# First attention of a four-layer kernel: value bias folded into the output bias, weights rounded on GpSimd, sixteen unread products between the halves of the norm

## The chip, the cores and the metric

The kernel runs on one core of a Trainium2 chip. The metric is the device time of one execution in microseconds. The kernel is timed in runs of its own, and one more execution is recorded by the profiler; times inside the kernel are counted from the start of the span of that execution.

## The reference

Four layers run one after the other, each with a layer norm before it and a residual sum behind it. Only the first matters here:

```python
x = x + attn0(layernorm(x), Wqkv, bqkv, Wo, bo)      # x: 1024 x 512
x = x + ffn0(layernorm(x), w1, m1, w2, m2, w3, m3)   # base + mean(|w - base|) * sign(w - base)
x = x + attn1(...)                                    # 32 heads, index scores, top 128
x = x + ffn1(...)                                     # LoRA

def attn0(x, Wqkv, bqkv, Wo, bo):                     # one head of 128
    q, k, v = split(x @ Wqkv + bqkv)
    p = softmax(q @ k.T / sqrt(128))
    return (p @ v) @ Wo + bo
```

Since the rows of the softmax sum to one, the value bias adds `bv @ Wo` to every row of the result.

## The kernel before, in words

All matrix products are made to float32 accuracy by splitting each operand into a rounded part and a rest (`hi`, `lo`), and adding three products (`mm3`: L345, L346, L347 in order of issue). One operand pair costs two operations: the rounding (ScalarE, or a CAST on VectorE) and a subtraction (VectorE, L1086 in `split`, or GpSimd).

Five engine programs run side by side, each in its own written order, and meet through semaphores.

- SyncE loads x (8 tiles of 128 rows), the attention's weights and biases, and then 44 chunks of feed-forward weights, two loads to a chunk. The chunks go through a ring of four slots: a slot is loaded again when ScalarE is done with the chunk in it.
- GpSimd subtracts the base from each chunk (L582). It does nothing else up to the second layer.
- ScalarE takes the sign (L771) and the sum of absolute values (L773) of each chunk in `weight_chunk`. Between these it rounds the transposed tiles of the norm (L761), adds the query and key biases (L790), rounds the values (L818), takes the exponentials of the scores (L809) and rounds their transposes (L823).
- VectorE does the norm in two halves of four tiles (`first_norm`: statistics, a square root on ScalarE at L779, then L1071 to L1079, then one scaling a tile at L1103), splits the projection weights tile by tile between these, takes the row maxima of the scores, and the rests of all operands. It also splits the output weights (`W0`) and adds the output bias to x (`B0`, `B4`).
- TensorE transposes the normed tiles (L1522), makes the query and key projections (4 groups of 12 products of 512 columns), then goes through `ATT_PE`: `S` a tile of scores, `V` a value tile (two bias products at L1539, then 12 of 128 columns), `T` the eight transposes of a tile of probabilities (L1584), `O` probabilities times values, `Y` the output projection. Before `T7` it waits until ScalarE has done 28 chunks (L1568), since the sum over these scales the first feed-forward weights.

The three lists `ATT_PE`, `ATT_ACT` and `ATT_DVE` are written by hand; in `ATT_ACT`, `Cn` stands for n weight chunks.

## Time and profile before

| | |
|---|---|
| three timed runs, median | 1443.37 us (1441.29 to 1444.63) |
| profiled execution | 1442.61 us |
| its span | 1440.8 us |
| TensorE busy | 1329.5 us (92%) |
| VectorE busy | 1107.4 us (77%) |
| ScalarE busy | 832.9 us (58%) |
| GpSimd busy | 641.7 us (45%) |

PE is TensorE's matmul stream, PEld its weight loads, DVE VectorE, ACT ScalarE, POOL GpSimd, SPq the queue that issues transfers. A row of the timeline has the start, the duration, engine, line, operation, what is written and read, and the count; in brackets stands the idle time before it and what ended it. [...] Busy time of pipelined matmuls overlaps, so the distance from one start to the next is the better measure of pace.

### The profile page before, as it was taken

To read this page: it belongs to the slowest core of one execution; us is meant where nothing else is said; L and a number is where in the kernel's file an instruction comes from. 1 tells how busy PE (TensorE), PEld (TensorE's weight loads), DVE (VectorE), ACT (ScalarE), POOL (GpSimd) and SP (SyncE) were. 2 spreads that over 40 slices of the span, in tenths; PEclk is the share of its full clock that TensorE was granted. 3 is DMA by queue.
4 is the path that set the end of the run, shared out by engine and by line. 5 is a ranking of instruction groups with operands and counts; after the bars stand their busy time and mean duration, and the time that the engine had idled before them with its cause. 6 is when DMAs were issued, how large, how long until landed. Compare 5 with 4: busy or idle time off the path is not lost.

```text
span 1440.8 us, 21299 instructions
## 1 busy us (share of the span) xinstructions
PE 1329.5 (92%) x7160; PEld 1107.8 (77%) x7160; DVE 1107.4 (77%) x2247; ACT 832.9 (58%) x1819; POOL 641.7 (45%) x630
## 2 busy tenths in 40 slices
PE   3988999999899689998769999999999999999998
PEld 2776888888789677776448888888888888888886
DVE  6567334443648499999979988988899889898976
ACT  4663542233246557774567667666776766677661
POOL 3520210010037445654665555556655655566534
PEclk9887999999999899998669999999999999999999
DMA  6630310000122334754830000000000000000021
GB/s 225 207 99 27 102 52 1 0 20 0 39 65 69 97 73 129 233 168 137 276 119 14 1 28 29 28 29 28 1 28 29 28 28 28 28 16 14 15 81 59
DMA packets 83722, 95.59 MB, mean 66 GB/s; under 512 B 11680, under 2 KB 59296, under 8 KB 83104
## 3 DMA queue, kind: packets, MB, share of 16 engines
q1 hardware_dynamic: 83616, 94.24, 20.9%
q8 instruction: 59, 0.97, 0.3%
q14 instruction: 47, 0.39, 0.1%
HBM read 75.34 MB, written 18.87 MB: 65 GB/s over the span
## 4 chain that ended last, share of the span: by engine, by line
PE 71%; DVE 16%; ACT 4%; issue 3%; DMA 2%; POOL 1%; SPq 1%; DVEq 0%; ACTq 0%
PE ps L345 17%; PE ps L347 16%; PE ps L346 16%; PE ps L1851 9%; PE ps L1871 3%; PE ps L1870 3%; DVE acc L1376 3%; DVE top L1387 2%; DVE xn_l L1449 1%; DVE rop L1399 1%; DVE acc L1390 1%; DVE rop L1397 1%; DVE pm L1429 1%; DVE rop L1398 1%; PE ps L1551 1%
## 5 line engine op out<-in xcount | busy, mean ns | idle before, releaser
L717 POOL TENSOR_SCALAR pm<-pm,smx 128x128 f32<-128x128 f32 (+1 forms) x255 | 188.8, 749 | 208.5 <-DVE smx L1436 208.5
L1024 ACT ACTIVATE pm<-pm,smx 128x128 f32<-128x128 f32 (+7 forms) x256 | 197.4, 773 | 35.5 <-DVE smx L1429 34.6
L1429 DVE CUSTOM_DVE_ANT_0 pm<-ps,mbias 128x128 f32<-128x128 f32 (+7 forms) x256 | 191.5, 752 | 29.0 <-PE ps L1851 13.4
L1851 PE MATMUL ps<-ident,pm 128*128 128x128 f32 x1152 | 174.8, 277 | 7.1 <-DVE pTa_l L1449 2.0
L1030 ACT ACTIVATE xn_h<-ps 128x512 fp32r<-128x512 f32 (+3 forms) x256 | 128.4, 512 | 84.5 <-PE ps L1851 81.5
L1449 DVE TENSOR_TENSOR xn_l<-ps,xn_h 128x512 fp32r<-128x512 f32 (+3 forms) x256 | 144.4, 587 | 24.2 <-ACT xn_h L1030 23.2
L345 PE MATMUL ps<-latT_l,qc_h 128*128 128x512 f32 (+3 forms) x384 | 143.1, 373 | 17.0 <-DVE smx L1429 8.9
L1851 PEld LDWEIGHTS ps<-ident,pm 128*128 128x128 f32 x1152 | 132.8, 141 | 32.9 <-issue 11.4
L347 PE MATMUL ps<-latT_h,qc_h 128*128 128x512 f32 (+3 forms) x384 | 134.0, 349 | 0.0
L346 PE MATMUL ps<-latT_h,qc_l 128*128 128x512 f32 (+3 forms) x384 | 133.6, 348 | 0.0
L1376 DVE SCALAR_TENSOR_TENSOR acc<-ps,iw,acc 128x768 f32<-128x768 f32 (+4 forms) x105 | 87.1, 875 | 25.3 <-ACT ps L910 25.1
L345 PEld LDWEIGHTS ps<-latT_l,qc_h 128*128 128x128 f32 x384 | 73.2, 191 | 34.0 <-issue 13.0
L678 POOL TENSOR_TENSOR rop<-rop 128x512 f32<-128x512 f32 x60 | 77.3, 1288 | 36.6 <-DVE rop L1399 36.6
L345 PE MATMUL ps<-xn_l,wc 128*128 128x512 f32 x224 | 91.9, 410 | 0.0
L582 POOL TENSOR_TENSOR wring<-wring,base 128x512 f32<-128x512 f32 (+1 forms) x33 | 43.1, 1309 | 108.4 <-DMA wring<-in_L_ffn_w 108.1
L1870 PE MATMUL ps<-xn_l,v 128*128 128x512 f32 (+3 forms) x256 | 91.3, 362 | 0.0
L1390 DVE MATCH_REPLACE8 acc<-top,acc 128x640 f32<-128x640 f32 (+4 forms) x112 | 89.7, 809 | 0.0
L346 PE MATMUL ps<-xn_h,wc 128*128 128x512 f32 x224 | 89.3, 399 | 0.0
L347 PE MATMUL ps<-xn_h,wc 128*128 128x512 f32 x224 | 89.2, 398 | 0.0
L910 ACT ACTIVATE ps<-ps 128x640 f32<-128x640 f32 (+4 forms) x112 | 73.9, 690 | 26.2 <-PE ps L347 26.0
L345 PE MATMUL ps<-ikT_l,iqT_h 128*128 128x512 f32 (+3 forms) x176 | 66.1, 376 | 23.3 <-DVE acc L1376 22.1
L1871 PE MATMUL ps<-xn_h,v 128*128 128x512 f32 (+3 forms) x256 | 87.0, 358 | 0.0
(287 smaller groups left out, 3742.6 us busy)
## 6 DMA issues: line engine op xcount, KB each, us to landing
iwq_raw<-in_L_attn_idx_wq_w SPq DMA_DIRECT2D x48, 256.0 KB, 3.3
base<-in_L_ffn_mean_w SPq DMA_DIRECT2D x28, 256.0 KB, 3.2
wring<-in_L_ffn_w SPq DMA_DIRECT2D x21, 256.0 KB, 3.6
ow_raw<-in_L_attn_o_w SPq DMA_DIRECT2D x8, 512.0 KB, 4.0
xn_t<-in_L_attn_o_w SPq DMA_DIRECT2D x8, 512.0 KB, 4.1
wuvo<-pr_even SPq DMA_DIRECT2D x8, 512.0 KB, 5.2
wuvo<-pr_hl SPq DMA_DIRECT2D x8, 512.0 KB, 4.8
wuvo_h<-wuvo SPq DMA_DIRECT2D x16, 256.0 KB, 2.7
```

The costliest lines, as they stand in the source:

```text
L345: pe.matmul(dst, lh, rl, start=start, stop=False)
L346: pe.matmul(dst, ll, rh, start=False, stop=False)
L347: return pe.matmul(dst, lh, rh, start=False, stop=stop)
L717: pool.tensor_scalar(pm[:, i % 4, 0:w], pm[:, i % 4, 0:w], smx[:, 32 + i:33 + i], 0.0, ALU.mult, ALU.add).then_inc(hd_p, 1)
L1024: act.activation(pm[:, i % 4, 0:w], pm[:, i % 4, 0:w], ACT.Exp, bias=smx[:, i:i + 1], scale=-1.0, accum_out=smx[:, 16 + i:17 + i]).then_in ...
L1030: act.activation(dst[:, 4 * c:4 * c + nk, tile(tq % 4)], ps[:, t_bank(p, i), 0:nk * P].rearrange("p (k s) -> p k s", k=nk), COPY).then_inc ...
L1376: dve.scalar_tensor_tensor(acc_of(t), score(n, t), w, acc_of(t), ALU.mult, ALU.add)\
L1429: dve.tensor_tensor_reduce(out=pm[:, i % 4, 0:w], in0=two_banks(2 * (i % 2), w), in1=mbias[:, TRI[t]:TRI[t + 1]], scale=1.0, scalar=3.0 * BIG,
L1449: dve.tensor_tensor(dl[at], ps[:, t_bank(p, i), 0:nk * P].rearrange("p (k s) -> p k s", k=nk), f(dh[at]), ALU.subtract).then_inc(hd_lo, 1)
L1851: done = pe.transpose(ps[:, t_bank(p, i), tile(k)], pm[:, tq % 4, tile(4 * c + k)], ident[:])
L1870: pe.matmul(ps[:, 6, q], v, pl[:, k, q], start=k == 0, stop=False)
L1871: done = pe.matmul(ps[:, 6, q], v, ph[:, k, q], start=False, stop=k == nk - 1)
```

## The change

- The value bias is no longer put into the value tiles. GpSimd spreads it over 128 columns and splits it; TensorE multiplies it with the output weights (`Z0`, three products into bank 5), and VectorE adds the result to `bo_bc` (`B0`). The rows of x get that sum from GpSimd, in two runs of four additions before chunks 16 and 20.
- The projection weights and output weights are split on GpSimd, before chunks 4 and 7.
- The query and key projections are rounded by ScalarE from PSUM straight into `qkT_h`, and VectorE takes the rest with one operation from PSUM.
- Between tiles 3 and 4 of the norm, TensorE makes sixteen products of 512 columns into bank 7 that nothing reads.
- ScalarE does four chunks behind tile 3 and two behind tile 7 (before: one behind each of tiles 3 to 7), three instead of nine before the scores, and 19 instead of 14 in `ATT_ACT`.

```diff
@@ -78,10 +78,12 @@
     return [(step[0], int(step[1:])) for step in order.split()]
 
 
-ATT_PE = items("S0 S1 V0 V1 V2 V3 S2 V4 V5 V6 V7 T0 S3 T1 S4 T2 S5 T3 S6 O0 T4 S7 Y0 Y1 T5 Y2 T6 Y3 T7 O1 "
+ATT_PE = items("S0 S1 V0 V1 V2 V3 Z0 S2 V4 V5 V6 V7 T0 S3 T1 S4 T2 S5 T3 S6 O0 T4 S7 Y0 Y1 T5 Y2 T6 Y3 T7 O1 "
                "Y4 Y5 Y6 Y7")
-ATT_ACT = items("S0 S1 C2 V0 C2 S2 C1 V1 T0 C1 T1 S3 T2 S4 C1 T3 S5 C1 S6 C3 O0 T4 C1 S7 T5 C1 T6 C1 T7 O1")
-ATT_DVE = items("S0 S1 W0 V0 S2 B0 V1 T0 S3 T1 S4 T2 S5 T3 S6 B4 O0 T4 S7 Y0 Y1 T5 Y2 T6 Y3 T7 O1 Y4 Y5 Y6 Y7")
+ATT_ACT = items("C1 S0 S1 C2 V0 C1 S2 C2 V1 T0 C1 T1 S3 C1 T2 S4 C1 T3 S5 C2 S6 C2 O0 T4 C1 S7 C1 T5 C2 T6 C2 T7 O1")
+ATT_DVE = items("S0 S1 V0 B0 S2 V1 T0 S3 T1 S4 T2 S5 T3 S6 O0 T4 S7 Y0 Y1 T5 Y2 T6 Y3 T7 O1 Y4 Y5 Y6 Y7")
+FIRST_CHUNKS = {3: 4, 7: 2}
+ADD_AT = {16: 0, 20: 4}
 
 
 
@@ -418,8 +425,7 @@
             sp.dma_start(attn_raw[:, 0:NK * 3 * D0].rearrange("p (k n) -> p k n", k=NK),
                          wqkv.rearrange("(k p) n -> p k n", p=P)).then_inc(ld_a, 16)
             with nc.allow_non_contiguous_dma(reason="a small bias column"):
-                sp.dma_start(bq_col[:], bqkv[0:2 * D0].rearrange("(a p) -> p a", p=P)).then_inc(ld_a, 16)
-            sp.dma_start(bv_bc[:], row(bqkv[2 * D0:3 * D0], D0)).then_inc(ld_a, 16)
+                sp.dma_start(bq_col[:], bqkv.rearrange("(a p) -> p a", p=P)).then_inc(ld_a, 16)
             sp.dma_start(attn_raw[:, NK * 3 * D0:], wo).then_inc(ld_a, 16)
             sp.dma_start(bo_bc[:], row(bo, HID)).then_inc(ld_a, 16)
 
@@ -435,7 +441,7 @@
                     c = slice((s % 4) * 448, (s % 4) * 448 + 448)
                     ws, ms = rows[:, s // 4, c], mrows[:, s // 4, c]
                 if chunk == 2 * NI:
-                    sp.wait_ge(at_w, 2)
+                    sp.wait_ge(at_wo, 1)
                     sp.wait_ge(at_proj, 6)
                     sp.wait_ge(at_b, 2)
                 number, last, _ = RING[chunk]
@@ -575,9 +581,39 @@
                                pattern=[[-1, P]], channel_multiplier=1)
             pool.drain().then_inc(consts, 1)
 
+            def first_weights():
+                pool.wait_ge(ld_a, 64)
+                for k in range(NK):
+                    pool.tensor_copy(wqkv_h[:, k, :], raw[:, k, :])
+                pool.drain()
+                for k in range(NK):
+                    pool.tensor_tensor(wqkv_l[:, k, :], raw[:, k, :], f(wqkv_h[:, k, :]), ALU.subtract)
+                pool.drain().then_inc(at_w, 1)
+
+            def output_weights():
+                pool.tensor_copy(wo_h[:], attn_raw[:, NK * 3 * D0:])
+                pool.tensor_scalar(bv_f[:], ones[:], bq_col[:, 2:3], 0.0, ALU.mult, ALU.add)
+                pool.drain()
+                pool.tensor_tensor(wo_l[:], attn_raw[:, NK * 3 * D0:], f(wo_h[:]), ALU.subtract).then_inc(at_wo, 1)
+                pool.tensor_copy(bv_h[:], bv_f[:])
+                pool.drain()
+                pool.tensor_tensor(bv_l[:], bv_f[:], f(bv_h[:]), ALU.subtract).then_inc(at_bv, 1)
+
+            def bias_rows(first):
+                pool.wait_ge(at_zb, 1)
+                for t in range(first, first + 4):
+                    pool.tensor_tensor(xt(t), xt(t), bo_bc[:], ALU.add)
+                pool.drain().then_inc(at_b, 1)
+
             for chunk in range(WCHUNKS):
                 m, s, width = wt_chunk(chunk)
                 slot = ring(chunk)
+                if chunk == 4:
+                    first_weights()
+                elif chunk == 7:
+                    output_weights()
+                if chunk in ADD_AT:
+                    bias_rows(ADD_AT[chunk])
                 pool.wait_ge(ld_w[RING[chunk][0]], 32 * (RING[chunk][2] + 1))
                 pool.tensor_tensor(slot, slot, base[m][:, s * width:(s + 1) * width], ALU.subtract).then_inc(wt_d, 1)
 
@@ -779,20 +815,15 @@
                 act.activation(rs_sqrt[:, c], rs_var[:, c], ACT.Sqrt).then_inc(at_rs, 1)
                 for t in range(4 * half, 4 * half + 4):
                     norm_hi(0, t)
-                    if t >= 3:
+                    for _ in range(FIRST_CHUNKS.get(t, 0)):
                         weight_chunk()
-            for _ in range(4):
-                weight_chunk()
             for u in range(4):
+                m, n = divmod(u, 2)
                 act.wait_ge(at_proj, u + 1)
-                if u >= 2:
-                    act.wait_ge(at_qkv, u - 1)
-                act.activation(xn_t[:, u % 2, :], ps[:, u, :], ACT.Identity,
-                               bias=bq_col[:, u // 2:u // 2 + 1]).then_inc(at_q, 1)
-                if u < 2:
+                act.activation(qkT_h[:, m, 512 * n:512 * n + 512], ps[:, u, :], ACT.Identity,
+                               bias=bq_col[:, m:m + 1]).then_inc(at_q, 1)
+                if u < 3:
                     weight_chunk()
-            for _ in range(3):
-                weight_chunk()
 
             def weight_hi(g, k):
                 act.wait_ge(ff_tr, 2 * g + k + 1)
@@ -1111,8 +1142,6 @@
                 dve.tensor_scalar(rs_var[:, first:first + n], mv[:, first:first + n, 1], EPS, None, ALU.add)
                 rsqrt(k, n, first)
 
-            raw = attn_raw[:, 0:NK * 3 * D0].rearrange("p (k n) -> p k n", k=NK)
-
             def first_norm(half):
                 c = slice(4 * half, 4 * half + 4)
                 dve.wait_ge(ld_x[half], 64)
@@ -1136,17 +1165,14 @@
             for t in range(4, NT):
                 norm_scale(0, t)
                 norm_lo(0, t - 1)
-                if t == 4:
-                    dve.wait_ge(ld_a, 80)
-                split(wqkv_h[:, t - 4, :], wqkv_l[:, t - 4, :], raw[:, t - 4, :])
             norm_lo(0, NT - 1)
-            dve.drain().then_inc(at_w, 1)
             for u in range(4):
                 m, n = divmod(u, 2)
                 c = slice(512 * n, 512 * n + 512)
                 dve.wait_ge(at_q, u + 1)
-                split(qkT_h[:, m, c], qkT_l[:, m, c], xn_t[:, u % 2, :])
-                dve.drain().then_inc(at_qkv, 1)
+                dve.scalar_tensor_tensor(qkT_l[:, m, c], ps[:, u, :], bq_col[:, m:m + 1], f(qkT_h[:, m, c]),
+                                         ALU.add, ALU.subtract).then_inc(at_qkv, 1)
+
             def values(b):
                 dve.wait_ge(at_vhi, b + 1)
                 dve.tensor_tensor(v_l[:, 4 * b:4 * b + 4, :], ps[:, 6 + b, :].rearrange("p (k s) -> p k s", k=4),
@@ -1181,14 +1207,9 @@
                 if kind == "V":
                     values(i)
                     continue
-                if kind == "W":
-                    split(wo_h[:], wo_l[:], attn_raw[:, NK * 3 * D0:])
-                    dve.drain().then_inc(at_w, 1)
-                    continue
                 if kind == "B":
-                    for t in range(i, i + 4):
-                        dve.tensor_tensor(xt(t), xt(t), bo_bc[:], ALU.add)
-                    dve.drain().then_inc(at_b, 1)
+                    dve.wait_ge(at_z, 1)
+                    dve.tensor_tensor(bo_bc[:], bo_bc[:], ps[:, 5, :], ALU.add).then_inc(at_zb, 1)
                     continue
                 if kind == "O" and i == 1:
                     dve.wait_ge(wt_tot, 1)
@@ -1222,6 +1243,7 @@
                         for t in range(4):
                             norm_lo(1, t)
                 else:
+                    dve.wait_ge(at_b, i // 4 + 1)
                     dve.wait_ge(at_y, i + 1)
                     dve.scalar_tensor_tensor(xt(i), ps[:, 7 - i % 2, :], sm0[:, 3 * NT + i:3 * NT + i + 1], xt(i),
                                              ALU.mult, ALU.add).then_inc(at_x, 1)
@@ -1524,6 +1546,10 @@
 
             for t in range(NT):
                 norm_tile(0, t)
+                if t == 3:
+                    pe.wait_ge(ln_hi, 4)
+                    for _ in range(16):
+                        pe.matmul(ps[:, 7, :], xn_h[:, 0, 0:P], xn_h[:, 0, 0:512], start=True, stop=True)
             pe.wait_ge(ln_lo, NT)
             pe.wait_ge(at_w, 1)
             for u in range(4):
@@ -1536,10 +1562,9 @@
 
             def value_tile(t):
                 dst = ps[:, 6 + t // 4, tile(t % 4)]
-                pe.matmul(dst, ones[0:1, :], bv_bc[0:1, :], start=True, stop=False)
                 for k in range(NK):
                     last = mm3(pe, dst, xn_h[:, k, tile(t)], xn_l[:, k, tile(t)],
-                               wqkv_h[:, k, tile(2)], wqkv_l[:, k, tile(2)], False, k == NK - 1)
+                               wqkv_h[:, k, tile(2)], wqkv_l[:, k, tile(2)], k == 0, k == NK - 1)
                 if t % 4 == 3:
                     last.then_inc(at_proj, 1)
 
@@ -1561,6 +1586,11 @@
             for kind, i in ATT_PE:
                 if kind == "V":
                     value_tile(i)
+                    continue
+                if kind == "Z":
+                    pe.wait_ge(at_wo, 1)
+                    pe.wait_ge(at_bv, 1)
+                    mm3(pe, ps[:, 5, :], bv_h[:], bv_l[:], wo_h[:], wo_l[:], True, True).then_inc(at_z, 1)
                     continue
                 if kind == "T" and i == 7:
                     pe.wait_ge(wt_abs, 2 * NI)
@@ -1580,6 +1610,8 @@
                     pe.wait_ge(at_exp, i + 1)
                     for c in range(2):
                         reach(pe, at_lo, 2 * i + c - 1 if i else 0)
+                        if i == 0 and c == 1:
+                            pe.wait_ge(at_zb, 1)
                         for k in range(4):
                             last = pe.transpose(ps[:, 4 + c, tile(k)], p0[:, i % 3, tile(4 * c + k)], ident[:])
                         last.then_inc(at_tr, 1)
@@ -1601,8 +1633,6 @@
                             norm_tile(1, t)
                 else:
                     pe.wait_ge(at_ot, i // 4 + 1)
-                    if i == 0:
-                        pe.wait_ge(at_w, 2)
                     if i >= 2:
                         pe.wait_ge(at_x, i - 1)
                     mm3(pe, ps[:, 7 - i % 2, :], oT[:, 0, tile(i % 4)], oT[:, 1, tile(i % 4)], wo_h[:], wo_l[:],
```

## Rows read from the trace of the kernel before

**Rows 1.** Stretches of the span by stage: engines' busy time, clock, transfers.

```profile
49.68:78.00 28.32, 28.32 (x131) 24.57 (x132) 11.13 (x13) 14.28 (x29) 11.84 (x9) 0.66 0.49 149
78.00:109.63 31.63, 25.88 (x124) 19.99 (x122) 24.16 (x37) 26.28 (x53) 9.04 (x7) 0.88 0.41 126
...
128.00:380.00 252.00, 247.99 (x1152) 202.53 (x1151) 102.33 (x162) 85.55 (x167) 19.45 (x14) 0.99 0.09 25
```

**Rows 2.** Timeline from 17 to 34 us, all engines.

```profile
17.65 0.62 ACT L771 ACTIVATE sgn<-wring 128x512 int8<-128x512 f32 x1
...
19.60 1.26 POOL L582 TENSOR_TENSOR row_bc<-row_bc,base 128x512 f32<-128x512 f32 x1
...
20.33 0.56 DVE L1125 TENSOR_SCALAR rs_var<-mv 128x4 f32<-128x4 f32 x1
20.95 0.21 ACT L779 ACTIVATE rs_sqrt<-rs_var 128x4 f32<-128x4 f32 x1 [1.89 <-DVEq L1126]
...
30.69 1.27 POOL L582 TENSOR_TENSOR wring<-wring,base 128x512 f32<-128x512 f32 x1 [7.04 <-DMA wring<-in_L_ffn_w]
30.81 1.56 DVE L1086 TENSOR_TENSOR wqkv_l<-attn_raw,wqkv_h 128x384 fp32r<-128x384 f32 x1
...
31.65 0.62 ACT L771 ACTIVATE sgn<-wring 128x512 int8<-128x512 f32 x1
...
33.16 0.63 ACT L771 ACTIVATE sgn<-wring 128x512 int8<-128x512 f32 x1
33.17 0.77 PE L345 MATMUL ps<-xn_l,wqkv_h 128*128 128x512 f32 x1 [2.17 <-DVEq L1143]
```

**Rows 3.** Timeline of TensorE in the value tiles, at either clock.

```profile
52.62 0.48 PE L1539 MATMUL ps<-bv_bc,ones 1*128 1x128 f32 x2
...
53.03 0.33 PE L345 MATMUL ps<-wqkv_l,xn_h 128*128 128x128 f32 x1
...
54.31 0.27 PE L347 MATMUL ps<-wqkv_h,xn_h 128*128 128x128 f32 x1
...
71.00 0.79 PE L1539 MATMUL ps<-bv_bc,ones 1*128 1x128 f32 x2
...
74.47 0.79 PE L1539 MATMUL ps<-bv_bc,ones 1*128 1x128 f32 x2
```

**Rows 4.** Short stretches around changes of TensorE's pace and clock.

```profile
34.97:38.38 3.41, 3.41 (x9) 2.65 (x8) 0.00 (x0) 2.41 (x6) 2.27 (x2) 1.00 0.92 308
38.40:41.80 3.40, 3.40 (x16) 2.74 (x15) 1.00 (x2) 2.98 (x6) 2.33 (x3) 1.00 0.84 303
45.22:48.63 3.41, 1.75 (x8) 1.08 (x6) 3.10 (x4) 1.55 (x3) 1.49 (x2) 1.00 0.69 199
...
55.47:58.86 3.39, 3.39 (x27) 3.01 (x26) 1.64 (x2) 3.04 (x8) 2.62 (x2) 1.00 0.25 66
58.90:62.27 3.37, 3.37 (x15) 3.18 (x16) 0.15 (x1) 0.87 (x3) 1.28 (x1) 0.50 0.85 285
```

**Rows 5.** Timeline of TensorE where it waits for the chunks.

```profile
109.63 0.63 PE L1568 MATMUL ps<-absum,ones 128*128 128x28 f32 x2 [1.13 <-ACTq L774]
```

**Rows 6.** VectorE's groups by form, 22 to 50 us: busy us, mean ns, idle before.

```profile
L1086 DVE TENSOR_TENSOR wqkv_l<-attn_raw,wqkv_h 128x384 fp32r<-128x384 f32 x4 | 3.2, 808 | 0.3
...
L1084 DVE CAST wqkv_h<-attn_raw 128x384 fp32r<-128x384 f32 x4 | 1.4, 348 | 0.0
```

**Rows 7.** GpSimd's groups by form: busy us, mean ns, idle before.

```profile
L629 POOL CAST v<-latn 128x512 fp32r<-128x512 f32 x1 | 0.6, 613 | 0.0
```

**Rows 8.** ScalarE's groups by form, 78 to 109.63 us.

```profile
L823 ACT ACTIVATE xn_h<-ps 128x512 fp32r<-128x512 f32 x14 | 7.7, 596 | 2.3 <-PE ps L1584 1.9
L809 ACT ACTIVATE p<-ps,sm 128x1024 f32<-128x1024 f32 x5 | 5.6, 1116 | 1.4 <-DVE sm L1208 1.3
...
L809 ACT ACTIVATION_READ_ACCUMULATOR p<-ps,sm 128x1 f32 x5 | 1.0, 200 | 0.0
```

**Rows 9.** Timeline of TensorE in front of the first scores.

```profile
49.68 0.50 PE L345 MATMUL ps<-qkT_l,qkT_h 128*128 128x512 f32 x1 [2.71 <-DVEq L1149]
```

More of the change, by code:

```diff
@@ L184, in build @@
         wqkv_l = sbin(q_scope, "wqkv_l", [P, NK, 3 * D0], F32R)
+        bv_f = sbin(q_scope, "bv_f", [P, D0])
+        bv_h = sbin(q_scope, "bv_h", [P, D0], F32R)
+        bv_l = sbin(q_scope, "bv_l", [P, D0], F32R)
         q_scope.close()
@@ L194, in build @@
         v_l = sbin(a_scope, "v_l", [P, NT, D0], F32R)
-        bq_col = sbin(a_scope, "bq_col", [P, 2])
-        bv_bc = sbin(a_scope, "bv_bc", [P, D0])
+        bq_col = sbin(a_scope, "bq_col", [P, 3])
         wo_h = sbin(a_scope, "wo_h", [P, HID], F32R)
@@ L304, in build @@
         at_rv, at_rs, at_w, at_proj, at_q, at_qkv, at_vhi, at_v, at_b = sems("at_", "rv rs w proj q qkv vhi v b")
+        at_wo, at_bv, at_z, at_zb = sems("at_", "wo bv z zb")
         at_s, at_max, at_exp, at_tr, at_hi, at_lo = sems("at_", "s max exp tr hi lo")
@@ L353, in xt @@
             return x[:, t * HID:(t + 1) * HID]
+        raw = attn_raw[:, 0:NK * 3 * D0].rearrange("p (k n) -> p k n", k=NK)
         def two_banks(b, w=1024):
```

## The prediction

> **What bounds the kernel now.** I read the stages first [rows 1]: is TensorE full, and at which clock? From 128 to 380 us it is busy 247.99 of 252.00 us: behind the first attention it has no slack, so whatever the attention gives or takes by 128 us moves the end one for one. The change lies wholly before that. There the reader sees three things: the first projection starts only at 33.17 us [rows 2]; from 49.68 to 78.00 it is always busy but at a mean granted clock of 0.66; and from 78.00 to 109.63 it has gaps while ScalarE is busy 26.28 of 31.63 us.
>
> I then read the starting stage as a timeline [rows 2], the value tiles product by product [rows 3] and the clock in short stretches [rows 4]. The attention's tail hangs on the place where TensorE waits for ScalarE's 28th weight chunk, 109.63 [rows 5]. That wait, in front of the last score transposes (T7), is my meter: everything behind it is the same in both kernels, so its shift is the sum.
>
> **Part 1: the start, up to the first projection (before: 33.17).** Three edits meet here.
>
> ScalarE now does four chunks before the second half's square root. A chunk takes 1.51 us (31.65 to 33.16), the first starts at 17.65, so the root comes at 17.65 + 4 x 1.51 = 23.7 instead of 20.95: 2.75 later. Their subtractions on GpSimd are ready (the fourth ends at 20.86) [rows 2].
>
> VectorE loses four splits of the projection weights, one behind each tile: a cast of 0.35 and a subtraction of 0.56 when it isn't held up (3.2 us for four, one of which took 1.56) [rows 2, 6]. Since part of a split covered the trip through TensorE and ScalarE, I take 0.75 off for each, 3.0, and 0.2 for the wait of the last. Root to projection was 33.17 - 20.95 = 12.2, so 9.0 without them: 32.7 if nothing else happens.
>
> GpSimd takes the splits. Its cast of 512 columns takes 0.613 us, its subtraction of 512 columns 1.26 [rows 2, 7]; for 384 columns I estimate 0.5 and 1.0. Four of each are 6.0 us, with the gaps 6.5, from 20.9 to about 27.5; then chunks 4 to 6 (1.27 each) and the split of the output weights keep it busy without a pause to about 35. So the weights are ready before the tiles; but VectorE pays: with GpSimd busy from 19.60 to 20.86, a 4-column VectorE operation stands from 20.33 to 20.89, 0.56 us, and a split's subtraction begun at 30.81 takes 1.56 while GpSimd runs from 30.69 to 31.96 [rows 2]. It waits for the running GpSimd operation to end. Behind the square root there are eight such operations: four of the five of the reciprocal root (I leave out the reciprocal) and four scalings. The root's four wait about 3.0 in all, the first scaling 1.2, the other three 0.4 to 0.5 each, of which half is hidden: 4.9. Bounds: nothing (32.7), or a whole 1.27 each, 10.2 (42.9). I take 4.9, as the rows show the wait twice: the projections start at 37.6, **4.4 us later**.
>
> [...]
>
> The sixteen unread products start when tile 3 is rounded, 17.8. At the pace of 34.97 to 38.38 (8 products begun in 3.41 us) they take 6.8 us, to 24.6; the next transposes are not due before 25.8, so they delay nothing. What they could give is the pace of the first projection products: the stretch to 38.38 runs at half the pace of the next (9 against 16 products) [rows 4]. [...] But between their end and 37.6 there are over ten microseconds with sixteen short transposes, and the 32 transposes of before had not raised the clock by 33.17. I count nothing; bound, 12 products x 0.2 = 2.4 gained.
>
> **Part 2: projections to scores.** The 48 products are the same, 13.8 us (33.17 to 49.68, less the wait at its end). Behind them ScalarE rounds straight from PSUM (0.6 to 0.7; an eviction of 512 columns takes 0.60 [rows 8]) and VectorE subtracts once, without a cast and with one SBUF operand, so it does not wait; 0.75, an estimate. Before, TensorE stood 2.71 us in front of S0 [rows 9]; now 0.7 + 0.75 + 0.1. Gain 1.1. S0 starts at 53.0, 3.3 late.
>
> **Part 3: value tiles.** The bias pair costs 0.41 before the products (52.62 to 53.03); eleven products start between 53.03 and 54.31, so twelve take 1.40. At the lower clock a tile with its pair takes 3.47 (71.00 to 74.47) [rows 3]. Does the clock still fall? It stood at 1.00 from 55.47 to 58.86, a stretch of nothing but value tiles with their pairs, and at 0.50 from 58.90 on; it did not fall behind 45.22 to 48.63, where TensorE did 512-column products for half the time and then nothing [rows 4]. Without pairs a tile comes 1.40 behind the last instead of 1.90, and Z0, S2 and their 512-column products stand between the two fours. No row of before shows such tiles; between the two cases I lean to the one that kept its clock, since the fours are denser and dense products stand on both sides of each. Then the sixth semaphore count of the projections is there at 53.0 + 2.75 (S0, S1) + 5.6 + 0.7 (Z0) + 1.4 (S2) + 5.6 = 69.0, where before it was 74.47 + 3.3 = 77.8. Bound from the other side: V4 to V7 at half pace, 4.9 more, and up to 2.6 for V0 to V3.
>
> **Part 4: ScalarE becomes the bound.** From 49.68 to 78.00 it was busy 14.28 of 28.32 us, since the value tiles kept it waiting [rows 1]; that goes. But the new order leaves 18 chunks behind S0, where 14 were. From the first exponential (3.1 behind S0's start, 56.1) to the 28th chunk it has eight exponentials of 1.12 and an accumulator read of 0.20 (10.5), 18 chunks (27.2), fourteen evictions for T0 to T6 at 0.60, overlapping a little (7.7), three single ones (1.8): 47.2, and waits, which I put at 2.3 (S2's maximum, queued on VectorE behind V0 and the bias sum, 1.5; S7's, 0.8) [rows 8]. Sum 105.6, against 109.6: **4.0 us gained**. Check on before, 78.00 to 109.63: five exponentials 6.6, nine chunks 13.6, the fourteen evictions 7.7, two single ones 1.2 make 29.1 of 31.63 us, so 2.5 of waits [rows 1]: mine for the new order are of that size.
>
> What runs beside it and costs nothing: VectorE loses 8 additions and the output-weight split; GpSimd gains two runs of four additions (5.3 each). By the hand count chunk 16, behind the first run, is ready at 75.1 when ScalarE wants it at 75.4; cover is thin there, so each microsecond more on GpSimd is a microsecond of ScalarE. The products of O0 have 1.7 us of cover. I take 0.4 off the gain for these two: **-3.6 us**. Profiled before: 1442.61 (span 1440.8), which is 0.8 under the median 1443.37; so 1439.0 on its scale and **1439.8** on the median's.
>
> **The rivals.** 0.2% is 2.9 us, about what the measurement can tell.
> 1. *Forecast*, 0.50: 1439.8, own range 1437 to 1443.
> 2. *VectorE is hardly held up at the start*, 0.17: gain up to 4.9 more, 1435. For it: the 4-column operations are short and might slip into GpSimd's gaps. Against: both rows above.
> 3. *The unread products keep the clock*, 0.05: 2.4 more, 1437.4. For: they come right before the second half. Against: the sparse transposes behind them. [...]
> 4. *The clock falls in the value tiles all the same*, 0.13, the case on the other side: V4 to V7, S2, T0, S3 at half pace are 4.9 + 1.2 + 1 + 1.2 later, less 1.3 of ScalarE's slack: T7 at 112.6, +3.0; with V0 to V3 in it, +5.6: 1446.4 to 1449. For it: the tiles are the same sparse kind, and no row shows them without pairs. It decides once the last value tile ends later than about 76.
> 5. *ScalarE starves*, 0.15: the additions on GpSimd come too late, or the clock falls in the sparse stretch before O0 (from 78.00 to 109.63 it was 0.88 in the mean [rows 1]) and O0's 24 products run 3 us longer; +2 to +4 on the forecast, 1442 to 1444: no difference.
>
> The start's upper bound, 42.9, puts T7 at 110.9, 1.3 behind before: it alone makes no case of slower. Range: leaving out the tails of 2 and 4, 1434.0 to 1447.5. Faster: 0.31 of case 1, 0.17, 0.05, together 0.53; slower: 0.13 and 0.03 of case 5, 0.16; same: the rest, 0.31.
>
> **What the new profile should show.** Right: the second square root at 23.7; VectorE's small operations stretched to about 1 us; first projection near 37.6 at half pace; eight value tiles 1.4 us apart at clock 1.00; ScalarE with hardly a gap from 56 to 106; the 28th chunk at 105 to 107. Wrong: a start near 33 (case 2); a clock of 0.50 between 58 and 76 (case 4); ScalarE waiting on GpSimd's subtractions about chunks 16 and 20 (case 5). My prediction fails most easily on the start, whose two bounds lie ten microseconds apart.

## The result, and the profile after

The changed kernel takes 1438.78 us (median of 20 runs, 1436.60 to 1442.02); the kernel before, in 20 runs beside it, 1442.28 (1435.95 to 1449.22). The ratio is 0.9975, with a 95% interval of 0.9965 to 0.9985: **faster by 0.25%, 3.5 us**. Forecast were 1439.8 us and a gain of 3.6. The profiled execution took 1436.89 us, its span 1435.1.

Its tail, the 28th chunk and its sum, is 5.07 us earlier than in [rows 5]. The timeline of TensorE in the changed kernel, at the wait in front of T7:

```profile
104.56 0.63 PE L1598 MATMUL ps<-absum,ones 128*128 128x28 f32 x2 [3.74 <-ACTq L810]
```

The same stretches as in [rows 1], with the one ahead of them. A row has the length of the stretch, each engine's busy time with its number of instructions (PE, PEld, DVE, ACT, POOL), TensorE's mean granted clock (1.00 is full), and the transfers' share and rate in GB/s:

```profile
33.17:49.68 16.51, 15.10 (x52) 11.69 (x53) 4.60 (x7) 9.22 (x19) 5.81 (x6) 0.72 0.40 119
49.68:78.00 28.32, 25.09 (x170) 21.53 (x169) 13.28 (x21) 22.96 (x46) 16.93 (x15) 1.00 0.53 166
78.00:109.63 31.63, 20.13 (x89) 15.53 (x88) 17.02 (x31) 25.57 (x52) 18.28 (x16) 0.86 0.58 181
...
128.00:380.00 252.00, 247.52 (x1155) 202.29 (x1154) 104.72 (x158) 85.13 (x166) 18.57 (x14) 0.99 0.08 25
```

In the value stretch the clock is 1.00 instead of 0.66, and ScalarE is busy for 22.96 us instead of 14.28. Behind 128 us TensorE is as full as before (247.52 us of 252.00, against 247.99).

The start, as a timeline of all engines, to be read beside [rows 2]:

```profile
18.34 0.62 ACT L807 ACTIVATE sgn<-wring 128x512 int8<-128x512 f32 x1
18.50 5.14 PEld L1552 LDWEIGHTS ps<-xn_h 128*128 128x128 f32 x16 [1.09 <-ACT xn_h L797]
18.50 5.58 PE L1552 MATMUL ps<-xn_h 128*128 128x512 f32 x16 [0.69 <-ACT xn_h L797]
...
22.32 3.90 POOL L590 TENSOR_TENSOR wqkv_l<-attn_raw,wqkv_h 128x384 fp32r<-128x384 f32 x4
...
24.43 0.20 ACT L815 ACTIVATE rs_sqrt<-rs_var 128x4 f32<-128x4 f32 x1
24.66 0.18 DVE L1102 RECIPROCAL rs_out<-rs_sqrt 128x4 f32<-128x4 f32 x1 [3.83 <-ACT rs_sqrt L815]
...
24.92 0.37 DVE L1104 TENSOR_TENSOR rs_tmp<-rs_out 128x4 f32<-128x4 f32 x1
25.36 0.88 DVE L1106 TENSOR_TENSOR rs_tmp<-rs_tmp,rs_var 128x4 f32<-128x4 f32 x1
26.31 0.17 DVE L1108 TENSOR_SCALAR rs_tmp<-rs_tmp 128x4 f32<-128x4 f32 x1
26.39 3.89 POOL L618 TENSOR_TENSOR wring<-wring,base 128x512 f32<-128x512 f32 x3 [0.18 <-issue]
26.55 1.12 DVE L1110 TENSOR_TENSOR rs_out<-rs_out,rs_tmp 128x4 f32<-128x4 f32 x1
27.75 1.41 DVE L1134 TENSOR_SCALAR xn_t<-x,mv,rs_out 128x512 f32<-128x512 f32 x1
29.07 0.68 DVE L1128 TENSOR_TENSOR xn_l<-ps,xn_h 128x512 fp32r<-128x512 f32 x1
...
29.67 0.89 DVE L1134 TENSOR_SCALAR xn_t<-x,mv,rs_out 128x512 f32<-128x512 f32 x1
...
31.59 1.48 DVE L1134 TENSOR_SCALAR xn_t<-x,mv,rs_out 128x512 f32<-128x512 f32 x1
...
33.37 0.46 POOL L600 TENSOR_TENSOR bv_l<-bv_f,bv_h 128x128 fp32r<-128x128 f32 x1
33.60 0.53 DVE L1134 TENSOR_SCALAR xn_t<-x,mv,rs_out 128x512 f32<-128x512 f32 x1
33.78 1.48 POOL L618 TENSOR_TENSOR row_bc<-row_bc,base 128x512 f32<-128x512 f32 x1
...
36.72 0.79 PE L350 MATMUL ps<-xn_l,wqkv_h 128*128 128x512 f32 x1 [1.41 <-DVE xn_l L1128]
```

The first projection starts 3.55 us later. Three of the root's small operations (0.37, 0.88 and 1.12 us, where 0.16 is the free duration) and three of the four scalings (1.41, 0.89 and 1.48, where it is 0.54) are stretched while GpSimd works beside them. The fourth scaling takes its free duration, 0.53 us, though a short GpSimd operation (33.37 to 33.83) runs beside its beginning. GpSimd's own subtraction of 512 columns at 33.78, begun while that scaling runs, takes 1.48 us, against 1.26 to 1.28 in [rows 2] and in the kernel before at 34.75.

TensorE from the scores to the unfolded bias product Z0:

```profile
52.36 0.50 PE L350 MATMUL ps<-qkT_l,qkT_h 128*128 128x512 f32 x1 [1.57 <-DVE qkT_l L1173]
...
55.24 0.22 PE L350 MATMUL ps<-wqkv_l,xn_h 128*128 128x128 f32 x1
...
60.55 0.45 PE L350 MATMUL ps<-wo_l,bv_h 128*128 128x512 f32 x1
```

The gap in front of the scores is 1.57 us, against 2.71 in [rows 9]. Four value tiles take 60.55 - 55.24 = 5.31, so 1.33 us each; in [rows 3] one took 3.47 us at half clock, and at full clock 1.90 (from the pair at 52.62 to the next at 54.52, 0.41 of it ahead of the first product). Three stretches of the changed kernel, in the columns of [rows 4]:

```profile
55.24:67.99 12.75, 12.75 (x106) 12.35 (x105) 4.08 (x8) 10.07 (x20) 5.09 (x5) 1.00 0.41 134
22.00:28.90 6.90, 2.08 (x9) 1.31 (x7) 3.86 (x6) 2.30 (x7) 6.58 (x8) 1.00 0.76 259
28.90:42.50 13.60, 10.18 (x30) 7.38 (x31) 6.19 (x9) 5.24 (x11) 7.35 (x8) 0.50 0.26 77
```

All eight value tiles run at 1.00. At the start the pace doubles at 22.0, in the middle of the unread products: eight of them start in the 3.50 us from 18.5, the other eight by 23.7. The clock column says 1.00 on both sides of that point, and up to 28.9 us; then it falls to 0.50 and is back only at 42.5, 5.8 us behind the first projection. Before, the pace doubles at 38.4, 5.2 behind it; there, too, the column says 1.00 on both sides [rows 4], so what the rows show of this change is the pace.

ScalarE's groups by form between the first exponential and the 28th chunk, in the columns of [rows 8]:

```profile
L840 ACT ACTIVATE p<-ps,sm 128x1024 f32<-128x1024 f32 x8 | 8.9, 1118 | 4.3 <-DVE sm L1229 4.2
L809 ACT ACTIVATE wring<-wring 128x512 f32<-128x512 f32 x13 | 8.2, 632 | 1.2 <-issue 0.4
...
L854 ACT ACTIVATE xn_h<-ps 128x512 fp32r<-128x512 f32 x14 | 7.6, 596 | 0.5
...
L809 ACT ACTIVATE row_bc<-row_bc 128x512 f32<-128x512 f32 x5 | 3.2, 631 | 0.4
```

Eight exponentials, 18 chunks (13 in the ring, 5 in the row buffer) and fourteen evictions, as counted. Real waits are in front of exponentials only: 4.3 us, of which 1.34 stand ahead of the first.

### The profile page after: what moved, and what is told of

Read it like the earlier page. It is cut to its first block, busy times and chain, and to the rows that moved or that the text cites. A ratio compares the mean times of both kernels' runs of the same rounds, so it can differ in the third digit from the quotient of the medians.

```text
span 1435.1 us, 21299 instructions
## 1 busy us (share of the span) xinstructions
PE 1318.9 (92%) x7163; PEld 1098.9 (77%) x7163; DVE 1093.6 (76%) x2226; ACT 832.5 (58%) x1819; POOL 658.1 (46%) x651
## 4 chain that ended last, share of the span: by engine, by line
PE 68%; DVE 17%; ACT 5%; issue 3%; DMA 2%; SPq 2%; POOL 1%; ACTq 0%; DVEq 0%
PE ps L350 16%; PE ps L352 15%; PE ps L351 15%; PE ps L1881 9%; PE ps L1901 3%; DVE acc L1398 3%; PE ps L1900 3%; DVE top L1409 2%; DVE xn_l L1471 1%; DVE rop L1421 1%; DVE acc L1412 1%; DVE rop L1419 1%; DVE pm L1451 1%; DMA iwq_raw<-in_L_attn_idx_wq_w 1%; DVE rop L1420 1%
```

## The experiments

Each was compared with the kernel before on the same chip. Its medians there were 1442.69 us (experiments 1 to 4), 1444.34 (5 to 8) and 1441.75 (9 to 11); ratios are against these, with 95% intervals. The three groups ran on three chips: between groups, and against the changed kernel, the ratios are the safer comparison, since the medians of the kernel before differ by 2.6 us between the groups.

**1. The kernel before without the bias pair.** The value bias is left out.

```diff
             def value_tile(t):
                 dst = ps[:, 6 + t // 4, tile(t % 4)]
-                pe.matmul(dst, ones[0:1, :], bv_bc[0:1, :], start=True, stop=False)
                 for k in range(NK):
                     last = mm3(pe, dst, xn_h[:, k, tile(t)], xn_l[:, k, tile(t)],
-                               wqkv_h[:, k, tile(2)], wqkv_l[:, k, tile(2)], False, k == NK - 1)
+                               wqkv_h[:, k, tile(2)], wqkv_l[:, k, tile(2)], k == 0, k == NK - 1)
```

> The kernel before with nothing changed but that the two bias products of each value tile are left out, so the value bias is missing from the output. Theory of the prediction (the pairs cost the clock): value tiles 1.40 us apart at clock 1.00, the 28th chunk at about 97 to 100 us instead of 109.6, 9 to 12 us faster than before, which is more than the whole change gave (3.5). Rival (the clock falls in the value tiles with or without pairs, and the change gained by moving VectorE's work): clock 0.50 from about 59 us, gain at most 2 to 4 us.

Measured: 1428.16 us, ratio 0.9904 (0.9887 to 0.9921), so 14.5 us less. Its first scores, a stretch of its value tiles, and its wait in front of T7:

```profile
50.36 0.50 PE L345 MATMUL ps<-qkT_l,qkT_h 128*128 128x512 f32 x1 [3.86 <-DVEq L1149]
```

```profile
54.81:66.20 11.39, 11.39 (x98) 11.14 (x96) 7.96 (x11) 9.54 (x20) 5.32 (x4) 1.00 0.49 142
```

```profile
96.96 0.41 PE L1567 MATMUL ps<-absum,ones 128*128 128x28 f32 x2 [1.92 <-ACTq L774]
```

Behind the gap of 3.86 us in front of the scores the clock is at 0.50 from 51.0 to 54.3, a fall that the kernel before did not have; from there to T7 it is at 1.00, through all eight value tiles. Taking sixteen one-row operations out moves the 28th chunk by 12.7 us. Their own time at full clock would be 8 x (1.90 - 1.33) = 4.6 us, so by this estimate most of it is the clock. **The 14.5 us are four times what the whole change brings**, and more than the 9 to 12 that I had expected.

**2. The changed kernel with a pair again**, on a row of zeros, before the products of each value tile.

```diff
+            pool.memset(zero_row[:], 0.0)
...
+                pe.matmul(dst, ones[0:1, :], zero_row[0:1, :], start=True, stop=False)
                 for k in range(NK):
```

> The changed kernel with a pair of products put back in front of each value tile; it multiplies a row of zeros, so nothing is added. Theory: the clock falls to 0.50 in the value tiles again, the last value tile ends 6 to 10 us later, the 28th chunk at 110 to 113 us instead of 104.6, 6 to 8 us slower than the changed kernel (about 1445, ratio to before 1.002 to 1.004). Rival (pairs cost only their own 0.5 us a tile): clock 1.00, 0 to 2 us slower than the changed kernel.

Measured: 1447.62 us, ratio 1.0037 (1.0019 to 1.0055): 8.8 above the changed kernel, a little over the 6 to 8 expected. The 28th chunk is at 112.20. Its value stretch in four pieces:

```profile
54.57:61.77 7.20, 7.20 (x55) 6.50 (x54) 1.44 (x3) 5.12 (x10) 1.28 (x1) 1.00 0.28 86
61.77:65.20 3.43, 3.43 (x12) 2.85 (x11) 1.38 (x2) 1.84 (x4) 2.04 (x2) 0.51 0.53 153
65.20:72.10 6.90, 6.90 (x48) 5.79 (x48) 1.38 (x2) 3.91 (x8) 6.72 (x6) 0.99 0.38 103
72.10:78.90 6.80, 6.80 (x27) 6.11 (x28) 2.07 (x3) 3.04 (x6) 2.57 (x3) 0.50 0.43 129
```

TensorE shows no idle time in any of them, and its clock falls twice all the same. The pair is all that differs between these rows and the 12.75 us at 1.00 of the changed kernel. Why such a stream brings the clock down is not shown.

**3. The changed kernel without the sixteen unread products.**

```diff
-                if t == 3:
-                    pe.wait_ge(ln_hi, 4)
-                    for _ in range(16):
-                        pe.matmul(ps[:, 7, :], xn_h[:, 0, 0:P], xn_h[:, 0, 0:512], start=True, stop=True)
```

> The changed kernel without the sixteen unread products. Theory (they bring nothing, since the clock stood at 0.50 again when the projections began in the changed kernel): same time as the changed kernel within 0.5 us, ratio to before 0.9975. Rival (in most runs they shorten the slow start of the projections): 1 to 2.5 us slower than the changed kernel.

Measured: 1436.81 us, ratio 0.9961 (0.9947 to 0.9974), which overlaps the interval of the changed kernel. The pace of the projection products doubles at 42.4 us (0.43 us from start to start ahead of it, 0.23 behind it), where the clock came up at 42.5 with the unread products, and the 28th chunk is at 104.7 instead of 104.6. The products bring nothing.

**4. The changed kernel with the start of before**: projection weights split on VectorE between the tiles, one chunk behind each of tiles 3 to 6.

```diff
-FIRST_CHUNKS = {3: 4, 7: 2}
+FIRST_CHUNKS = {3: 1, 4: 1, 5: 1, 6: 1, 7: 2}
...
-                if chunk == 4:
-                    first_weights()
-                elif chunk == 7:
+                if chunk == 7:
...
                 norm_lo(0, t - 1)
+                split(wqkv_h[:, t - 4, :], wqkv_l[:, t - 4, :], raw[:, t - 4, :])
```

> The changed kernel with the start of before: the projection weights split on VectorE between the tiles, and one chunk behind each of tiles 3 to 6, two behind tile 7. Theory (the start was lost to a late square root and to VectorE held up by GpSimd): projections at 33 to 34 instead of 36.7, the 28th chunk 2.5 to 3.5 us earlier than 104.6, about 3 us faster than the changed kernel, ratio to before 0.9955. Rival (ScalarE's list is the bound wherever it begins): 0 to 0.5 us.

Measured: 1434.78 us, ratio 0.9951 (0.9933 to 0.9968), 4.0 under the changed kernel (3.5 by the ratios). First projection at 32.69, scores at 47.13, 28th chunk at 99.33, so 4.03, 5.23 and 5.23 us earlier: the start's delay goes through to the 28th chunk in full, and the time shows the larger part of it.

**5. As experiment 4, with ScalarE's lists of before** (14 chunks in front of the scores instead of 10, and 14 behind them instead of 18), without the unread products.

```diff
-ATT_ACT = items("C1 S0 S1 C2 V0 C1 S2 C2 V1 T0 C1 T1 S3 C1 T2 S4 C1 T3 S5 C2 S6 C2 O0 T4 C1 S7 C1 T5 C2 T6 C2 T7 O1")
+ATT_ACT = items("C2 S0 S1 C2 V0 C2 S2 C1 V1 T0 C1 T1 S3 T2 S4 C1 T3 S5 C1 S6 C3 O0 T4 C1 S7 T5 C1 T6 C1 T7 O1")
...
-FIRST_CHUNKS = {3: 1, 4: 1, 5: 1, 6: 1, 7: 2}
+FIRST_CHUNKS = {3: 1, 4: 1, 5: 1, 6: 1, 7: 5}
```

> The changed kernel with all but the bias path taken back as far as it concerns ScalarE's chunks and the start: projection weights split on VectorE, ScalarE's chunk lists of before (14 of 28 chunks ahead of the first scores instead of 10), no unread products. It keeps the folded bias, the output weights and the additions on GpSimd, and the short rounding of the projections. Theory (the pairs' removal gave 14.5 us, the late start took about 3 back and the four chunks moved behind S0 about 6): projections at 33 to 34, S0 at 48 to 49, the 28th chunk at 94 to 97, 1425 to 1429 us, ratio to before 0.988 to 0.991. Rival (what was taken back is the cost of the fold itself: Z0, the additions on GpSimd in front of chunks 16 and 20): the 28th chunk at 100 or later, 1432 or more.

Measured: 1432.69 us, ratio 0.9929 (0.9907 to 0.9951), with the 28th chunk at 103.48. I had set it at 94 to 97, since four chunks fewer behind the scores, at 1.51 us each, are worth 6 us; what came is the rival that I had named, at 100 or later. The timeline of ScalarE, and then that of GpSimd, show where it went:

```profile
57.98 0.60 ACT L839 ACTIVATE v_h<-ps 128x512 fp32r<-128x512 f32 x1
66.45 0.63 ACT L797 ACTIVATE sgn<-wring 128x512 int8<-128x512 f32 x1 [7.87 <-POOL wring L608]
```

```profile
59.98 4.98 POOL L597 TENSOR_TENSOR x<-x,bo_bc 128x512 f32<-128x512 f32 x4 [6.89 <-DVE bo_bc L1206]
65.14 1.28 POOL L608 TENSOR_TENSOR wring<-wring,base 128x512 f32<-128x512 f32 x1 [0.18 <-issue]
```

GpSimd stands in front of chunk 16 for 6.89 us, until VectorE has summed the unfolded bias; then it adds for 4.98; only then comes the chunk for which ScalarE has waited 7.87. A second, smaller cost stands ahead of the scores: behind the split of the output weights on GpSimd, ScalarE waits 2.10 us for chunk 7 (at 38.07).

**6. The changed kernel with those two lists alone.** The edit is that of experiment 5, with GpSimd's splits and the unread products kept.

> The changed kernel with ScalarE's chunk lists of before alone; projection weights stay on GpSimd and the unread products stay. Theory: square root at 21, projections at 33 to 34.5 (root to projections stays 12.3), the 28th chunk at 96 to 98.5, 1428 to 1431 us. Rival (GpSimd's rounding sets the start: weights there only at 26 to 27 and VectorE held up more, since the root now falls among GpSimd's casts): projections at 35.5 or later, 1431 to 1434.

Measured: 1434.44 us, ratio 0.9941 (0.9923 to 0.9959). The square root is back at 20.48 us and the first projection at 31.91, 4.8 us earlier; yet the 28th chunk is at 104.59, since ScalarE waits 7.88 us for the same chunk behind the same additions. So the 1428 to 1431 us that I had expected were missed. The median is 4.3 us under the changed kernel's, though the chunk comes no earlier. Behind that wait the clock was at 0.50 from 107.3 to 110.8 here, and from 104.0 to 114.2 in the changed kernel, and the first feed-forward product starts at 121.95 against 124.01: 2.1 us. The rest no trace shows, since the profiled execution of this kernel took 1436.79 us, 2.4 above its median and as long as that of the changed kernel (1436.89).

**7. The changed kernel with the projection weights' split on VectorE alone**, four chunks in front of the root kept.

> The changed kernel with the projection weights split on VectorE again, chunk lists and unread products as changed. Theory (what VectorE saves on the splits it loses again by standing behind GpSimd's operations): root at 24.4, projections at 36.3 to 37, time as the changed kernel within 1 us, ratio 0.9970 to 0.9980. Rival (the splits' move is what helps or hurts at the start): projections 1.5 us or more away from 36.7.

Measured: 1441.48 us, ratio 0.9984 (0.9969 to 0.9999). Root to projection takes 13.4 us (25.00 to 38.40), 1.1 more than with the split on GpSimd (24.43 to 36.72). The projections are 1.7 us away from 36.7, which is the sign of the rival, but 0.6 of it is a later root. So the move of the split by itself is worth about a microsecond here, and what delays the start is the four chunks in front of the root: without them, in experiment 6, the first projection is at 31.91.

**8. Experiment 5 with the additions and the output-weight split on VectorE**, in the places that they had before.

```diff
-ATT_DVE = items("S0 S1 V0 B0 S2 V1 T0 S3 T1 S4 T2 S5 T3 S6 O0 T4 S7 Y0 Y1 T5 Y2 T6 Y3 T7 O1 Y4 Y5 Y6 Y7")
+ATT_DVE = items("S0 S1 W0 V0 B0 S2 A0 V1 T0 S3 T1 S4 T2 S5 T3 S6 A4 O0 T4 S7 Y0 Y1 T5 Y2 T6 Y3 T7 O1 Y4 Y5 Y6 Y7")
...
-ADD_AT = {16: 0, 20: 4}
+ADD_AT = {}
```

> As the kernel with the old lists, old start and folded bias, but the output weights are split and the residual rows added on VectorE again, so GpSimd gets only the small split of the value bias. Theory (VectorE has room once ScalarE is the bound): within 1.5 us of it, 1426 to 1430. Rival (GpSimd's additions are what relieves VectorE): 3 us or more slower than it.

Measured: **1423.51 us**, ratio 0.9872 (0.9846 to 0.9898): 9.2 under experiment 5, 15 under the changed kernel, and the fastest of all. I had expected no more than 1.5 us of difference to experiment 5, and the rival said slower: both were wrong. Its scores start at 47.50, 1.44 before those of experiment 5; the rest is gained behind them. Its wait in front of T7:

```profile
92.81 0.41 PE L1588 MATMUL ps<-absum,ones 128*128 128x28 f32 x2 [1.65 <-ACTq L790]
```

**9. The changed kernel, its own lists, with the additions alone on VectorE.** This and the next ask whether engine or place had cost the 9 us.

> The changed kernel with its own lists, but the two runs of four additions of the output bias to x back on VectorE (behind the maxima of S2 and of S6), none on GpSimd. My theory: in the changed kernel ScalarE never waited for a subtraction of GpSimd behind the first scores, since its list is late, so the additions there cost nothing: the 28th chunk stays at 104 to 105.5 us and the time at 1437 to 1441 us, the same as the changed kernel. Rival: additions on GpSimd cost by themselves, by contention between the two engines or through later loads, whatever the list: 28th chunk at 100 or before, 1430 to 1434 us.

Measured: 1439.08 us, ratio 0.9978 (0.9959 to 0.9997); the 28th chunk at 104.4. No difference to the changed kernel. With its late list ScalarE waits for no subtraction of GpSimd behind the scores, so the additions are covered, as forecast.

**10. Experiment 8 with the additions on GpSimd, in front of chunks 22 and 23.**

```diff
-ADD_AT = {}
+ADD_AT = {22: 0, 23: 4}
```

> The kernel of the run with 1423.5 us, but with the additions on GpSimd, in front of chunks 22 and 23 instead of 16 and 20 (the output weights stay split on VectorE). My theory: what cost 9 us between the last two kernels was the place, in front of chunk 16, where GpSimd stood behind the sum that comes from the unfolded bias product Z0, and ScalarE with it for 7.9 us; in front of chunks 22 and 23 the sum is long there and GpSimd had gaps of 2.1 and 4.5 us: 28th chunk at 92.5 to 95.5 us, 1423 to 1427 us. Rival: the engine costs, wherever the additions stand: 28th chunk at 99 or later, 1430 us or more.

Measured: 1424.58 us, ratio 0.9875 (0.9847 to 0.9904), the 28th chunk at 94.70. The timeline of GpSimd at the first run of additions:

```profile
67.54 5.04 POOL L595 TENSOR_TENSOR x<-x,bo_bc 128x512 f32<-128x512 f32 x4
72.75 1.29 POOL L606 TENSOR_TENSOR wring<-wring,base 128x512 f32<-128x512 f32 x1 [0.18 <-issue]
```

No wait stands in front of them. The same additions on the same engine, six and three chunks later, cost nothing that the time shows, though the 28th chunk is 1.9 us later than in experiment 8: it was the place that cost, not the engine. How much the place cost is less sharp. Against experiment 5 the output-weight split has moved as well, and the scores start 1.10 us earlier (47.84 against 48.94); of the 8.78 us at the 28th chunk 7.7 arise behind the scores, and these belong to the place.

**11. Experiment 8 with the sixteen unread products.**

> The kernel of the run with 1423.5 us and the sixteen unread products between tiles 3 and 4 added. My theory: their clock falls again before the projections (in the changed kernel it stood at 1.00 from 22.0 to 28.9 and came back at 42.5), so they bring nothing: first projection at 31.9 to 32.7 us, 28th chunk within 1 us of 92.8, 1422 to 1426 us. Rival: with a start at 32 only three microseconds lie between the fall and the projections, and the clock is back sooner: clock up at 33 to 34 instead of 36.2, 28th chunk 1.5 to 2 us earlier, 1420 to 1422 us.

Measured: 1426.59 us, ratio 0.9888 (0.9858 to 0.9917). The interval overlaps that of experiment 8; the first projection is at 32.68 and the 28th chunk at 93.32. The clock fell from 1.00 to 0.50 at 29.8 and was back at 36.6, not before the 36.2 at which the pace of the products doubles in experiment 8 (0.43 us from start to start ahead of it, 0.23 behind it). With the earlier start, too, they bring nothing. (The profiled execution took 1430.73 us, 8.2 more than that of experiment 8, with the 28th chunk only 0.5 later: the stages behind the attention differ by that much between two executions.)

## Why the prediction was right, by its own steps

**The start (forecast +4.4, measured +3.55).** The square root came at 24.43 instead of 23.7: the first chunk began at 18.34, not 17.65, since the rounding of the norm's fourth tile ahead of it came at 17.85, 0.7 later than in the trace of before. From root to projection I had 9.0 plus a hold-up of 4.9 = 13.9; it took 12.29. The rows of after give the hold-up over free durations of 0.16 and 0.54: 0.21 + 0.72 + 0 + 0.96 for the root's four operations, 0.87 + 0.35 + 0.94 + 0 for the scalings, together 4.05. But before had such an event of its own, a scaling of 1.52 us behind its root, which sat inside my 12.2. The kernel before:

```profile
21.44 0.16 DVE L1073 TENSOR_TENSOR rs_tmp<-rs_out 128x4 f32<-128x4 f32 x1
...
22.41 1.52 DVE L1103 TENSOR_SCALAR xn_t<-x,mv,rs_out 128x512 f32<-128x512 f32 x1
...
25.35 0.54 DVE L1103 TENSOR_SCALAR xn_t<-x,mv,rs_out 128x512 f32<-128x512 f32 x1
```

Net 3.1, near 12.29 - 9.0 = 3.3. So the hold-up was there, in six of the eight operations, and the term 1.6 too large: 1.0 because I had not searched the rows of before for the hold-up that was already paid, most of the rest because the eight operations lost 4.05 and not 4.9.

Not every operation of VectorE is held up. The subtraction from PSUM at 29.07 takes 0.68 us and the reciprocal at 24.66, which I had left out of the eight, 0.18, both while GpSimd runs; in the kernel before they took the same with GpSimd idle (0.68 at 23.85, 0.18 at 21.19). What sets the one kind apart from the other these runs do not show.

**The unread products (forecast nothing).** Right, by experiments 3 and 11. The clock was at 0.50 again when the projections began: the pace had doubled at 22.0, the clock fell at 28.9, near the end of a gap of 5.12 us, and behind that gap only sixteen transposes stand ahead of the projections. Rival 3 falls. What brings the clock down there is not shown. It fell ahead of the first of these transposes (29.21). In experiment 11 no gap around the transposes is above 1.31 us, and the clock fell at 29.8 all the same, with TensorE busy for 2.11 of the 5.80 us ahead of that.

**Projections to scores (forecast a gap of 1.55, measured 1.57).** Scores at 52.36 instead of 53.0, all of it from the start. VectorE's new subtraction, from PSUM, takes the estimated 0.75 us all four times, at 42.96 with GpSimd at work from 43.09 to 44.38 and at 45.95 with GpSimd idle; before, three of the four subtractions of two SBUF operands took 1.62 to 1.68 and the fourth 0.69.

**The value tiles (forecast 1.00 and 1.40 us each; measured 1.00 and 1.33).** This was the choice on which the sign hung, and experiments 1 and 2 show it from both sides: without the pair the kernel before keeps its clock in the value tiles (1.00 from 54.81 to 66.20), with a pair the changed kernel loses it (0.51 from 61.77, 0.50 from 72.10). My reason, that such tiles are denser and stand between dense products, was only a leaning, and no run tests it by itself. Rival 4 falls for the changed kernel; for a kernel that keeps the pair its price was nearly right: +3.0 to +5.6 on T7 was my estimate, and experiment 2 is at 112.20, +2.6 against before.

**ScalarE as the bound (forecast 105.6, measured 104.56).** From the first exponential to the 28th chunk I had 49.5 us; it took 104.56 - 55.54 = 49.02. The wait for S2's maximum was 1.40 (forecast 1.5), for S7's 1.28 (0.8). Rival 5's starving did not come: no wait for GpSimd, and experiment 9 shows the cover for the additions. Its other half did not come where I had put it: through O0, from 78 to 97 us, the clock was 1.00. It was 0.50 from 97.1 to 100.5 and from 104.0 to 114.2.

**Behind the meter (forecast: the same in both kernels).** This premise did not hold. Of the 5.07 us at T7 4.00 are left when the first feed-forward product starts (124.01; before 128.01). The kernel before, too, had a stretch at 0.50 there, from 106.7 to 116.9, but it ended 7.3 us behind T7, and that of the changed kernel ends 9.6 behind it. So the forecast gain of 3.6 met the measured 3.5 partly by luck: T7 moved by 5.07 instead of 4.0, and the 0.4 that I took off for thin cover was not needed, but a microsecond that the sum did not have was lost behind T7.

**Where the larger gain went.** The pair's removal is worth 14.5 us alone; the whole change brings 3.5. Experiment 1 has its scores at 50.36 and its 28th chunk at 96.96; after is 2.00 later at the scores and 7.60 later at the chunk. Four more chunks behind the scores at 1.51 are 6.0; with the 2.0 that is 8.0, against the 7.60. The prediction had both terms but set them against before, where the slow value tiles hid ScalarE's list, and so did not see that the chunk moves took back most of the fold. Experiments 4, 5 and 8 undo them one by one: 3.5 to 4.0 us for the start; the list of before gives its 6 only once the additions leave chunk 16.

Rival 2 (a start near 33) is refuted by the trace; 36.72 lies nearer to the forecast. One thing stays open. The value of the 28th chunk does not give the time to the microsecond: experiment 6 has it at 104.59, as after, and is 4 us faster in the median. The lower clock behind it, 3.5 against 10.2 us long, goes with 2.1 us at the first feed-forward product, about half. I have not tried what decides how long that stretch is, and the rest of the execution differs as well: from the first feed-forward product to the end the profiled executions take between 1309.6 us (experiment 8) and 1317.3 (experiment 11), with lower clocks at different places between 480 and 760 us (in pieces of 20 us the mean is 0.50 from 680 to 720 in experiment 8, but 0.63 and then 0.50 in experiment 11).

## What to carry to other kernels

When the slowest engine's clock depends on the stream that it is fed (here 1.00 without and 0.50 with a pair of one-row products in each value tile), look for odd operations in the stream before shortening anything else, and then re-read every list that was balanced against the slow stretch, since the next engine's work is no longer hidden: here 7.60 of the 12.7 us at the 28th chunk went back that way and at the start. A wait inside an in-order queue costs whatever stands behind it (GpSimd's 6.89 us in front of chunk 16, with its additions, were 7.87 us of ScalarE): put an addition that waits for another engine's sum only where that sum is long there, whichever engine does it. And before adding a contention term to a sum, check the baseline's rows for contention already paid, here 1.52 - 0.54 = 0.98 us.

## What the runs showed of the hardware that I had not expected

- Experiment 2 differs from the changed kernel by two one-row products ahead of the twelve of 128 rows in each value tile. Its clock was 1.00 from 54.57 to 61.77 us and 0.51 from there to 65.20, with no idle time of TensorE in the record (7.20 of 7.20 us and 3.43 of 3.43 busy), where the changed kernel had 1.00 from 55.24 to 67.99. The median was 8.8 us longer. The kernel before without its pairs, experiment 1, had 1.00 from 54.81 to 66.20, where the kernel before had 0.50 from 58.90 on, and was 14.5 us shorter. Both figures have the pairs' own time in them, 0.41 us of 1.90 for a tile of the kernel before.
- In the changed kernel, beside a running GpSimd, a 4-column product of two SBUF operands (L1110, at 26.55) took 1.12 us, against 0.16 in the kernel before with GpSimd idle (L1079, at 22.16); a 4-column reciprocal (at 24.66) took 0.18 beside GpSimd, as it did before without (at 21.19).
- Four additions of 512 columns took 5.02 us on GpSimd in the changed kernel (at 66.69), 4.98 in experiment 5 (at 59.98) and 5.04 in experiment 10 (at 67.54); the same four took 3.57 on VectorE in experiment 8 (at 59.74).
